# The first 1024 token rows are loaded during the last expert unit, and the wait for its added rows moves into the next stage

## The reference

```python
x = L0_attn_x
x = _layernorm(x + _L0_attn_ref(x, ...), axis=-1)
x = _layernorm(x + _L0_ffn_ref(x, ...), axis=-1)

# inside both: every token goes to its top 2 of 8 experts
h = jax.nn.gelu(xf[tok] @ W1[eid] + b1[eid], approximate=False) @ W2[eid] + b2[eid]
out = out.at[tok].add(gate[:, None] * h)
```

## Time and profile before

| | us |
|---|---|
| three timed runs, median (lowest to highest) | 1633.08 (1632.31 to 1634.97) |
| profiled execution, its own time | 1631.68 |
| its span, first to last instruction | 1629.9 |
| PE busy | 1520.2 (93%) |
| DVE busy | 1046.6 (64%) |
| POOL busy | 786.6 (48%) |
| ACT busy | 736.8 (45%) |
| mean granted TensorE clock | 0.956 of 2.4 GHz |

### The profile page before, as it was taken

The page is one execution under the profiler, slowest core; times in us unless marked ns, Lnnn a source line. Parts: engine busy times, 40 slices in busy tenths (PEclk is TensorE's granted clock), DMA queues, the critical chain, the costliest instruction groups (busy, mean ns, idle before and its releaser), DMA issues. The chain is left out here.

```text
span 1629.9 us, 37588 instructions
## 1 busy us (share of the span) xinstructions
PE 1520.2 (93%) x11761; PEld 1451.8 (89%) x11761; DVE 1046.6 (64%) x2953; ACT 736.8 (45%) x1698; POOL 786.6 (48%) x795
## 2 busy tenths in 40 slices
PE   6999996699999999999967999999999999999990
PEld 4777774699999999999866999999999999999990
DVE  5888886676766676676465655565565665565553
ACT  3555552454545455555344434434343434343324
POOL 3778884156656665665241334334334434434420
PEclk9999997599999999999985999999999999999995
DMA  7011010223433433342332132313213231411216
GB/s 245 33 35 35 32 36 33 93 44 93 98 62 78 99 92 50 91 126 42 89 138 94 33 104 33 107 29 86 56 26 107 36 103 27 113 30 27 34 19 212
DMA packets 63715, 119.07 MB, mean 73 GB/s; under 512 B 14384, under 2 KB 52784, under 8 KB 61488
## 3 DMA queue, kind: packets, MB, share of 16 engines
q0 software_dynamic: 35840, 42.38, 16.0%
q1 hardware_dynamic: 27824, 76.07, 12.8%
HBM read 79.71 MB, written 38.71 MB: 73 GB/s over the span
## 5 line engine op out<-in xcount | busy, mean ns | idle before, releaser
L855 POOL DMA_INDIRECT acc<-E_ysb,IDX x160 | 258.2, 1614 | 135.5 <-ACT E_ysb L945 66.3
L982 DVE TENSOR_TENSOR E_hraw<-E_sg,bank 128x256 f32<-128x256 f32 x320 | 134.6, 421 | 286.1 <-ACT E_sg L918 286.1
L850 POOL DMA_INDIRECT E_mg<-meta,IDX x160 | 150.9, 943 | 337.1 <-DVE E_gate L966 311.2
L1035 PE MATMUL bank<-E_xT,ws 128*128 128x256 f32 x960 | 272.4, 284 | 5.0 <-DVE E_xT L957 5.0
L1036 PE MATMUL bank<-E_xT,ws 128*128 128x256 f32 x960 | 271.9, 283 | 0.0
L1037 PE MATMUL bank<-E_xT,ws 128*128 128x256 f32 x960 | 271.7, 283 | 0.0
L993 DVE TENSOR_TENSOR E_hT<-E_hraw,E_hT 128x256 fp32r<-128x256 f32 x640 | 259.5, 416 | 0.0
L989 DVE CAST E_hT<-E_hraw 128x256 fp32r<-128x256 f32 x640 | 203.2, 318 | 58.5 <-ACT E_hraw L921 51.6
L918 ACT ACTIVATE E_sg<-bank 128x256 f32<-128x256 f32 x320 | 121.6, 384 | 256.4 <-PE bank L1037 254.6
L1035 PEld LDWEIGHTS bank<-E_xT,ws 128*128 128x128 f32 x960 | 183.2, 191 | 6.0 <-issue 5.8
L1035 PE MATMUL bank<-ws,E_hT 128*128 128x256 f32 x640 | 183.8, 287 | 0.0
(11 more groups left out here) (195 smaller groups left out, 4045.8 us busy)
## 6 DMA issues: line engine op xcount, KB each, us to landing
wraw<-in_w_ffn SPq DMA_DIRECT2D x8, 3072.0 KB, 10.5
wraw<-in_w_moe SPq DMA_DIRECT2D x8, 2048.0 KB, 8.0
X<-acc SPq DMA_DIRECT2D x16, 512.0 KB, 6.9
X<-in_x SPq DMA_DIRECT2D x8, 512.0 KB, 9.3
xn<-A_xn SPq DMA_DIRECT2D x32, 128.0 KB, 1.7
acc<-X SPq DMA_DIRECT2D x32, 128.0 KB, 1.7
acc<-X SPq DMA_DIRECT2D x8, 512.0 KB, 2.9
out<-C_xo SPq DMA_DIRECT2D x8, 512.0 KB, 2.8
```

The costliest lines, as they stand in the source:

```text
L850: nc.gpsimd.indirect_dma_start(out=mg[:, j, :], out_offset=None, in_=meta_dram, in_offset=at_slots(u, j)).then_inc(s_gm, 16)
L855: nc.gpsimd.indirect_dma_start(out=acc_dram, out_offset=at_slots(u, j), in_=ysb[:, j, :], in_offset=None, compute_op=ALU.add).then_inc(s_y ...
L982: V.tensor_tensor(hraw[:, f % RING, :], sg[:, f % RING, :], bank[f % RING][:, UW:2 * UW], ALU.mult).then_inc(s_hm, 1)
L1035: nc.tensor.matmul(out, wh, mh, start=first, stop=False)
```

## The change

SP's list in both expert stages gets three things at its end: a wait until all units but the last have landed in `acc`, and the loads of groups 0 and 1 (HEAD = 2, the first eight values of t, 1024 rows) into `X`. POOL's wait for the last unit is removed from the expert stages and stands as SP's first instruction in the next stage, ahead of the loads of groups 2 to 7. So that the last scatters may still be read from SBUF while the next stage runs, `ysb` and the semaphores become those of the whole program. The two filler runs on PE at the border of E1 and C1 are cut from 46 to 26 and from 12 to 4.

```diff
+G = 4
+GROUPS = NT // G
+HEAD = (UPE - 1) * UW // (G * P)
...
+            sp.wait_ge(s_ys, 16 * UT * (UNITS - 1))
+            for g in range(HEAD):
+                t = slice(g * G, (g + 1) * G)
+                sp.dma_start(X[:, t, :], by_partition(acc_dram)[:, t, :]).then_inc(s_head[g], 16)
...
                 pool.wait_ge(s_yb, UT * (u + 2))
                 add_rows(u)
-            pool.wait_ge(s_ys, 16 * UT * UNITS)
...
             if not glu:
-                keep_busy(nc, bank[7], ws[0], 46)
+                keep_busy(nc, bank[7], ws[0], 26)
...
-        s_ldx = [sem(f"ldx{g}") for g in range(GROUPS)]
+        s_ldx = s_head + [sem(f"ldx{g}") for g in range(HEAD, GROUPS)]
...
         @block.sync
         def _(sp):
-            for g in range(GROUPS):
+            sp.wait_ge(s_ys, 16 * UT * UNITS)
+            for g in range(HEAD, GROUPS):
                 t = slice(g * G, (g + 1) * G)
                 sp.dma_start(X[:, t, :], by_partition(io["acc1"])[:, t, :]).then_inc(s_ldx[g], 16)
...
-            keep_busy(nc, bank[7], ws0, 12)
+            keep_busy(nc, bank[7], ws0, 4)
...
         X = sb("X", [P, NT, D])
+        ysb = sb("ysb", [P, UT, D])
```

More of the change, by code:

```diff
@@ L756, in _, with expert_phase @@
             R.place(pe)
-def expert_phase(nc, bank, passed, io, tag, glu, IDX, scb, cst, wraw, ws):
+def expert_phase(nc, bank, passed, io, tag, glu, X, ysb, s_ys, s_head, IDX, scb, cst, wraw, ws):
     row_dram, acc_dram, meta_dram, w_dram = ((io["acc1"], io["acc2"], io["meta2"], io["w_ffn"]) if glu else
@@ L782, in expert_phase @@
         yraw = None if glu else sb("yraw", [P, UT, D])
-        ysb = sb("ysb", [P, UT, D])
         warm = sb("warm", [P, 1])
@@ L791, in expert_phase @@
         s_hm, s_xgn = (sem("hm"), sem("xgn")) if glu else (None, None)
-        s_y, s_ye, s_yb, s_yf, s_ys, s_wld, s_wh, s_wl = map(sem, ("y", "ye", "yb", "yf", "ys", "wld", "wh", "wl"))
+        s_y, s_ye, s_yb, s_yf, s_wld, s_wh, s_wl = map(sem, ("y", "ye", "yb", "yf", "wld", "wh", "wl"))
         s_pass_pe, s_pass_sp = passed["pe"], passed["sp"]
@@ L1075, in keep_busy, with between_phase @@
         nc.tensor.matmul(spare[:, :], w[:, 0, 0:P], w[:, 0, 0:4 * P], start=True, stop=True)
-G = 4
-GROUPS = NT // G
-def between_phase(nc, bank, io, X, IDX, cst, small, ws0):
+def between_phase(nc, bank, io, X, IDX, cst, small, ws0, s_ys, s_head):
     with ExitStack() as ctx:
@@ L1241, in _, with final_phase @@
             R.place(pe)
-def final_phase(nc, io, X, cst):
+def final_phase(nc, io, X, cst, s_ys, s_head):
     with ExitStack() as ctx:
@@ L1327, in build @@
         passed = {e: ctx.enter_context(nc.semaphore(f"passed_{e}")) for e in ("pool", "act", "pe", "sp")}
+        ys = [ctx.enter_context(nc.semaphore(f"ys{i}")) for i in range(2)]
+        head = [[ctx.enter_context(nc.semaphore(f"head{i}{g}")) for g in range(HEAD)] for i in range(2)]
         X = sb("X", [P, NT, D])
+        ysb = sb("ysb", [P, UT, D])
         IDX = sb("IDX", [P, SC], I32)
@@ L1338, in build @@
         with nc.sbuf_tensor("ws1a", [P, 2, 4096], F32R) as ws1:
-            expert_phase(nc, bank, passed, io, "E1", False, IDX, small["sc_moe"], cst, wraw, (ws0, ws1))
-        between_phase(nc, bank, io, X, IDX, cst, small, ws0)
+            expert_phase(nc, bank, passed, io, "E1", False, X, ysb, ys[0], head[0], IDX, small["sc_moe"], cst, wraw, (ws0, ws1))
+        between_phase(nc, bank, io, X, IDX, cst, small, ws0, ys[0], head[0])
         with nc.sbuf_tensor("ws1b", [P, 2, 6144], F32R) as ws1:
-            expert_phase(nc, bank, passed, io, "E2", True, IDX, small["sc_ffn"], cst, wraw, (ws0, ws1))
-        final_phase(nc, io, X, cst)
+            expert_phase(nc, bank, passed, io, "E2", True, X, ysb, ys[1], head[1], IDX, small["sc_ffn"], cst, wraw, (ws0, ws1))
+        final_phase(nc, io, X, cst, ys[1], head[1])
 def kernel(**inputs):
```

## The result

| us | before | changed |
|---|---|---|
| median of 4 timed runs | 1633.88 | 1623.55 |
| lowest to highest | 1632.31 to 1634.97 | 1620.19 to 1626.88 |
| profiled execution, its own time | 1631.68 | 1626.88 |
| its span | 1629.9 | 1625.1 |

The ratio is 0.994, with a 95% interval of 0.9926 to 0.9954: faster by 10.3 us.

A forecast was written before the change was run, and what follows sets the result against it. PE was busy 93% of the span, but at the borders the waits, DRAIN and first loads counted, then PE paced C1 and ACT C2. Gains 5.8 (C2) + 4.1 (C1) = 9.9 us; forecast 1623.3 us, range 1618.5 to 1628.

The forecast's parts named there:

- The DRAIN: POOL's queue at both expert-stage ends: fixed 3.73 us, starting at last issue's end; releases 2.3 and 2.1 us earlier.
- "long landed" rows: At both borders: DRAIN entries differ by 3 ns though all transfers had long landed, so its time is its own cost.
- Rival (a): POOL's border DRAIN waits for what is in flight, then takes 3.73 us; gain 5.5, time 1627.6 us; chance 0.16.
- Rival (b): POOL's border DRAIN shrinks to nothing; gain 15.6, time 1617.5 us; chance 0.07.
- The loads: Early loads late in the expert stages: in X before the release, 13 us of cover, cost 0.
- Rival (d): At both borders the release does not move and head loads are late; gain 1.8 us at most; chance 0.04.
- C2: Stage after E2: 3.7 us from no load wait plus 2.1 from the earlier release, 5.8 us gained.
- C1: Stage after E1: 2.3 us from the earlier release plus 1.8 net from fewer fillers, 4.1 us gained.
- the term of the clock: PE's restart in C1: low stretch of 3.3 us under load, costing 1.65 us, the same as before.
- The allowance of the step: Clock at PE's restart in C1: low stretch 2 us either way, so a cost of 0.65 to 2.65 us.
- Rival (c): C1 gives its part back through a longer low clock or late group 2 load; time 1627.3 us; chance 0.09.
- Rival (e): Slower: clock stays at 1.2 GHz through C1's tile loop, doubling its 28.3 us; time 1650 us; chance 0.04.

The follow-up runs named there:

- the repeat: The changed kernel itself, unaltered, run again beside variants with 26 and 4 fillers: 1623.25 us, ratio 0.9947 to the kernel before.

## Why the prediction came out right, and the term that was off

**The DRAIN (rivals a and b).** Forecast: its 3.73 us is a cost of its own and starts when the last issue is done, so the releases come 2.3 and 2.1 us earlier. The trace has it end 3.7 us behind the last issue at both borders, with the rows still in flight for two of them; the release moved by 2.5 and 2.3. The sign that was named for it, a DRAIN that starts 0.2 us behind the last issue and lasts 3.7, is not what the profile shows: it is entered ahead of the issues and lasts 7.4, and only its end agrees. The argument from "long landed" rows was also weaker than it sounded, since before they landed at 802.2 and the DRAIN started at 802.5. Rival (a), a DRAIN that first waits for the landing, would have left both where they were, and the moved wait alone excludes it. Rival (b), no DRAIN, would have released at once, not 3.9 us behind the last issue (its gain at C1 should have read 806.4 - 800.3 = 6.1, not 5.9).

**The loads.** Forecast: hidden, cost 0. They landed in at most 4.6 us, ahead of the scatters, so no run shows what a collision with these would cost. Rival (d) needed them late.

**C2.** Forecast 3.7 + 2.1 = 5.8, group 2 late by 0.3 and swallowed. Measured 5.9 in six traces, whatever the fillers (27.94 to 28.00 against 33.86), as 2.3 for the release and 3.6 for the load; group 2 late by 0.23, and no gap on ACT.

**C1.** Forecast 2.3 + 1.8 = 4.1; measured 2.8 in this trace, 3.6 and 2.9 in two others with 26 and 4 fillers. The release gave 2.5 and the way from it to the first transpose 1.7. That transpose stands 4.6 us behind the release, not about 3 as the prediction had it: the 3 counted the matmuls ahead of it at the full clock, against the low level that it assumed itself. The tile loop gave 1.4 back: from the first transpose to the selection chain it takes 841.18 - 811.39 = 29.8 us, where before took 28.3 and so did both kernels whose clock did not fall. The mechanism was there; the term of the clock was mis-sized. I took "the same again", a low stretch of 3.3 us from the restart on. (Before, the level fell only at 809.3, four fillers into the 12, and not right behind the small matmuls.) It was 6.7 us, of which 0.2 fell in the idle time, so it cost 6.5 / 2 = 3.25 under load instead of 1.65. That takes 1.6 off the forecast and leaves 2.5; the release gave 0.2 more; measured were 2.8. The allowance of the step went to 2.65. In the repeat the same 6.7 us began 2.0 us ahead of PE's restart, at 805.6, and cost 4.7 / 2 = 2.35: there C1 gave 3.6. That the low level can last twice as long as before was shown by the fillers cut alone, too.

On the clock I cited the Trainium skill (TensorE: Matmul & The Clock Gate, "Part 1: The HAM clock gate"). Its remark that the point of the change differs from run to run agrees with the traces of 40 fillers: 3.4, 0 and 0 us at the low level after the same 1.3 us of idle. The rule that speaks against cutting fillers holds here in part: cut alone they gave nothing in the time (0.9998), while together with the earlier release C1 is 1.6 to 2.4 us shorter with 26 and 4 than with 46 and 12.

**Rival (c)**, C1 gives its part back, came about to a third. **Rival (e)**, the low clock through the tile loop, did not occur: the longest low stretch at this border, with 10 fillers, was 10.2 us.

**The total.** Of the 9.9 us, 8.7 are in this pair of profiles and 9.0 in the mean of the three traces (3.1 + 5.9). The medians differ by 10.3, and by 9.9 in the repeat. That the forecast of 1623.3 stands 0.25 from the measured 1623.55 is partly chance: a term off by about 1 us is less than the runs scatter (1620.19 to 1626.88).

## What to carry to other kernels

A wait at a stage border costs its own length and pushes what stands behind it on the same queue; here a fixed 3.7 us DRAIN stood behind it, and moving the wait to the engine that needs the data, with a head start of loads whose rows are surely done, took 2.3 and 3.6 us off C2's start. Fillers that keep a clock up are sized against the release: with 46 they became the last at the barrier once the release came earlier, with 26 they left a gap of 4.5 us and a low clock that cost 2.4 to 3.3 us, and with 40, which end just ahead of POOL's DRAIN, C1 was shorter in all three traces. Measure stages from event to event, since a single profile of this kernel differed by 2.9 us in a stage that nobody had touched.

## What the runs showed that I had not expected

POOL's DRAIN behind indirect DMAs ended 3.7 us behind its entry when POOL was idle by then (3729 to 3732 ns, in the kernels with POOL's wait), and 3.7 us behind the last issue, or the memset after it, when entered before the last two scatters (7391 to 7397 ns, with the memset 7508). At C1's end, where POOL's last work is ordinary arithmetic, the DRAIN ended with that work: entered at 839.7, 2843 ns long, POOL's last instruction over at 842.5. Why the indirect DMAs leave 3.7 us behind is open.

C1's own end barrier took 0.3 us longer in the changed kernel. DVE's last instruction and ACT's first of E2, to be read with the earlier trace rows:

```profile
874.22 0.24 DVE L714 SCALAR_TENSOR_TENSOR IDX<-bank,R_free 128x80 int32<-128x80 f32 x1
875.03 1.28 ACT L895 ACT_TABLE_LOAD   x1 [5.72 <-PEq L1085]
```

0.57 us against 0.27, and POOL's two semaphore steps stand 0.4 us apart instead of 0.1. It is so in those traces in which POOL goes from its last scatter straight to the barrier, and not with POOL's wait kept, nor with the memset behind the scatters (steps at 872.8 and 872.8). The cause was not tested and stays open; it is the +0.3 in the table of stretches.
